# Three 128-row products of an FP32 token kernel split into 64-row halves, one image per PSUM bank

## The reference, cut to what matters

```
x = x + conv(group_norm(x))              # relu(info) * sigmoid(mask), 256 products, 1x1 conv
t = tokens(x)                            # 64 channels per token
q, k, v = ln(t) @ Wq, @ Wk, @ Wv         # norm 1: over 64 channels of a token
m = linear_attention(q, k, v) @ Wm       # 8 heads of 8
m = ln(m) * g1 + b1                      # norm 2
h = relu(cat(ln(t), m) @ W1) @ W2
t = t + ln(t) + ln(h) * g2 + b2          # norm 3
t = t + moe(ln(t))                       # norm 4; 8 experts, top 2, 64 -> 128 -> 64
```

## Time and profile before

| | |
|---|---|
| median of 3 runs | 1406.1 us (1400.49 to 1411.07) |
| the profiled execution | 1401.63 us, its span 1399.8 us |
| PE busy | 1227.9 us, 88% |
| DVE busy | 849.5 us, 61% |
| ACT busy | 736.9 us, 53% |
| POOL busy | 363.0 us, 26% |
| mean granted TensorE clock | 0.938 |

### The profile page before, as it was taken

How to read it: one execution, slowest core, us unless ns; L and a number is a source line. 1 busy time by engine, 2 the same in 40 slices (tenths; PEclk the granted TensorE clock), 3 DMA queues, 4 the chain that set the end, 5 groups by cost and what they waited for, 6 DMA issues and landing times.

```text
span 1399.8 us, 17533 instructions
## 1 busy us (share of the span) xinstructions
PE 1227.9 (88%) x6006; PEld 606.4 (43%) x6006; DVE 849.5 (61%) x1749; ACT 736.9 (53%) x982; POOL 363.0 (26%) x276
## 2 busy tenths in 40 slices
PE   5786799989999799987999988997889979999787
PEld 2565246434545237352373434643346434544111
DVE  6537665585548765567555876556665585547423
ACT  3442474654664556644556547464474554665433
POOL 0100132222323232222312223222241222323355
PEclk9987799989999799988999999998999989999999
DMA  2010561009310292003810066100661009210570
GB/s 91 31 31 1 124 151 34 13 1 199 92 46 1 56 204 61 16 2 79 195 47 16 1 135 155 31 16 3 145 145 40 7 1 205 55 46 1 113 162 15
DMA packets 15440, 96.67 MB, mean 69 GB/s; under 512 B 2672, under 2 KB 4720, under 8 KB 11120
## 3 DMA queue, kind: packets, MB, share of 16 engines
q1 hardware_dynamic: 15344, 95.46, 29.2%
HBM read 77.62 MB, written 9.44 MB: 62 GB/s over the span
## 4 chain that ended last, share of the span: by engine, by line
PE 50%; DMA 19%; DVE 11%; ACT 11%; issue 6%; SPq 2%; DVEq 0%; POOLq 0%; POOL 0%; ACTq 0%
DMA out<-XB 17%; PE HP L560 13%; PE R L455 9%; ACT H L677 8%; PE R L433 5%; PE YC L571 5%; PE R L513 5%; PE R L539 2%; PE R L492 2%; SPq L353 2%; PE R L520 2%; PE R L474 2%; PE R L483 2%; DMA CWB<-gates_hbm 1%; DVE TM L968 1%
## 5 line engine op out<-in xcount | busy, mean ns | idle before, releaser
L715 POOL TENSOR_TENSOR XB<-TM,XB 128x512 f32<-128x512 f32 x256 | 325.7, 1277 | 975.7 <-DVE TM L968 975.6
L677 ACT ACTIVATE H<-HP,W 128x1024 f32<-128x1024 f32 x256 | 285.7, 1116 | 352.9 <-PE HP L560 352.4
L560 PE MATMUL HP<-XF,W1E 64*128 64x512 f32 x1024 | 303.3, 670 | 38.8 <-ACT H L677 38.2
L968 DVE SCALAR_TENSOR_TENSOR TM<-YC,B2S,CWB 128x512 f32<-128x512 f32 x256 | 189.9, 747 | 196.4 <-PE YC L571 158.7
L571 PE MATMUL YC<-H,W 128*64 128x512 f32 x1024 | 292.2, 650 | 10.2 <-DVE TM L968 8.4
L560 PEld LDWEIGHTS HP<-XF,W1E 64*128 64x128 f32 x1024 | 80.1, 192 | 203.6 <-ACT H L677 165.4
L835 DVE TENSOR_REDUCE SM<-T 128x8 f32<-128x512 f32 x128 | 85.6, 684 | 111.4 <-ACT T L627 111.4
L571 PEld LDWEIGHTS YC<-H,W 128*64 128x64 f32 x1024 | 52.3, 139 | 209.3 <-issue 129.2
L433 PE MATMUL R<-W,T 128*128 128x128 f32 x768 | 100.2, 287 | 18.9 <-DVE T L845 18.9
L433 PEld LDWEIGHTS R<-W,T 128*128 128x128 f32 x768 | 89.4, 148 | 48.9 <-DVE T L845 42.4
L627 ACT ACTIVATE T<-R 128x512 f32<-128x512 f32 x128 | 73.8, 598 | 42.2 <-PE R L455 41.1
(11 more groups left out here) (96 smaller groups left out, 1371.5 us busy)
## 6 DMA issues: line engine op xcount, KB each, us to landing
CWB<-gates_hbm SPq DMA_DIRECT2D x32, 1536.0 KB, 26.4
CWB<-gates_hbm SPq DMA_DIRECT2D x32, 512.0 KB, 14.6
X<-x SPq DMA_DIRECT2D x16, 512.0 KB, 3.3
BIG<-XN SPq DMA_DIRECT2D x32, 256.0 KB, 3.8
out<-XB SPq DMA_DIRECT2D x16, 512.0 KB, 2.8
W<-wpack SPq DMA_DIRECT2D x1, 1176.0 KB, 7.2
gates_hbm<-CWR SPq DMA_DIRECT2D x16, 64.0 KB, 1.6
W1E<-w1e SPq DMA_DIRECT2D x1, 512.0 KB, 8.5
```

What stands on the lines that cost most here:

```text
L560: last = mm(HP[:, half(k)], W1E[img(k), e, :], XF[img(k), p, s, half(c)], start=True, stop=True)
L677: f(H[:, u % 2, :, :].rearrange("p k t -> p (k t)"), HP[:, :], ACT.Gelu, bias=col(B1E + e))\
L715: nc.gpsimd.tensor_tensor(acc, TM[:, u % 2, :], acc, ALU.add).then_inc(acc_done, 1)
L968: v.scalar_tensor_tensor(out=TM[:, u % 2, :], in0=YC[u % 2][:, :], scalar=B2S[:, e % 2, e // 2:e // 2 + 1], in1=CWB[:, s, e, half(c)], op0 ...
```

## The change

`by_token` at the three places is replaced by `image_tiles`. For each block of 128 tokens it makes two matmuls in place of one: 64 rows of the array (one image's channels) by 128 tokens, moving the 64 x 64 block of that image. Image 0's 64 columns go to the first bank of `R[s]`, image 1's to the second, block after block. Key and value keep `by_token`.

The layout in `R[s]` is then image by image, where it was block by block, so a bank is complete only when the whole slot is. PE therefore waits for both pieces of a slot before it starts, and signals both at its end. `scale_images` reads a bank (one image) and writes T1 in the old layout, in runs of 64 elements with a stride of 128; the transposes that follow, over both banks, wait for both of its operations. Norm 3 stays as it was.

```diff
+                def image_tiles(s, src, weights):
+                    for j in range(TB):
+                        for k in range(2):
+                            last = mm(R[s][:, CH * k + C * j:CH * k + C * j + C], src[img(k), s, P * j:P * j + P],
+                                      weights[img(k), img(k)], start=True, stop=True)
+                    return last
+
                 def centre_1():
-                    for s, c in PIECES:
-                        pe.wait_ge(x1_done, nth(a + 1, s, c))
-                        by_token(s, c, X, w("center")).then_inc(ln_ps, 1)
+                    for s in range(G):
+                        pe.wait_ge(x1_done, nth(a + 1, s, LAST))
+                        image_tiles(s, X, w("center")).then_inc(ln_ps, NCH)
...
                     for s, c in pieces(slots):
-                        pe.wait_ge(ln_tok, nth(a * LNS + k, s, c))
+                        if c == 0 or k == 3:
+                            pe.wait_ge(ln_tok, nth(a * LNS + k, s, c if k == 3 else LAST))
                         tokens(s, c, T1).then_inc(ln_back, 1)
...
                 def message():
-                    for s, c in PIECES:
-                        pe.wait_ge(att_done, nth(a + 1, s, c))
-                        by_token(s, c, T1, WMC[:, :]).then_inc(ln_ps, 1)
+                    for s in range(G):
+                        pe.wait_ge(att_done, nth(a + 1, s, LAST))
+                        image_tiles(s, T1, WMC).then_inc(ln_ps, NCH)
...
+                def scale_images(s):
+                    for k in range(2):
+                        v.tensor_tensor(T1[:, s, :].rearrange("p (j k c) -> p k j c", k=2, c=C)[:, k, :, :], norms(R[s][:, half(k)]),
+                                        SM[:, 3, s, some_norms(k)].unsqueeze(2)
+                                        .broadcast_to([P, NORMS // 2, C]), ALU.mult).then_inc(ln_tok, 1)
```

More of the change, by code:

```diff
@@ L529, in centre_4 @@
                 def centre_4():
-                    for s, c in PIECES:
-                        pe.wait_ge(x2_done, nth(a + 1, s, c))
-                        by_token(s, c, XB[:, par, :, :], w("center")).then_inc(ln_ps, 1)
+                    for s in range(G):
+                        pe.wait_ge(x2_done, nth(a + 1, s, LAST))
+                        image_tiles(s, XB[:, par, :, :], w("center")).then_inc(ln_ps, NCH)
                 def gates():
@@ L976, in parts @@
                     "conv_out": conv_out,
-                    "centre_1": lambda: squares(1), "rstd_1": lambda: rstd(1), "norm_1_0": lambda: scale(0), "norm_1_1": lambda: scale(1),
+                    "centre_1": lambda: squares(1), "rstd_1": lambda: rstd(1), "norm_1_0": lambda: scale_images(0), "norm_1_1": lambda: scale_images(1),
                     "query": lambda: elu_plus_one(1, Q), "key": lambda: elu_plus_one(2, K),
                     "key_value": key_value, "denominator": denominator, "numerator": numerator,
-                    "message": lambda: squares(2), "rstd_2": lambda: rstd(2), "norm_2_0": lambda: scale(0), "norm_2_1": lambda: scale(1),
+                    "message": lambda: squares(2), "rstd_2": lambda: rstd(2), "norm_2_0": lambda: scale_images(0), "norm_2_1": lambda: scale_images(1),
                     "tokens_3": lambda: squares(3), "rstd_3": lambda: rstd(3), "norm_3_0": lambda: scale(0), "norm_3_1": lambda: scale(1),
                     "features_3": features_3,
-                    "centre_4": lambda: squares(4), "rstd_4": lambda: rstd(4), "norm_4_0": lambda: scale(0), "norm_4_1": lambda: scale(1),
+                    "centre_4": lambda: squares(4), "rstd_4": lambda: rstd(4), "norm_4_0": lambda: scale_images(0), "norm_4_1": lambda: scale_images(1),
                     "gates": gates,
```

## The result

The changed kernel takes 1421.7 us (median of 4 runs, 1420.5 to 1427.9) against 1405.1 us before: a ratio of 1.0124, interval 1.0076 to 1.0173. Measured again beside the first experiments it was 1421.9 us, ratio 1.0104, interval 1.0084 to 1.0125. So it is 15 to 17 us slower. That is inside the forecast's range, but 12 us above the predicted time, and it is no "no change": both intervals lie wholly above 1, and both middles just beyond the 1% that the forecast drew as the line.

A forecast was written before the change was run, and what follows sets the result against it. Half of the span was PE, a fifth DMA; terms 0 + 0 + 1.2 + 3.9 + 0.5 + 1.1 = 6.7 us on 1401.6 gave 1408.3, on the median 1412.8, stated as 1410. Range 1396 to 1438.

The forecast's parts named there:

- the 1% that the forecast drew as the line: Whole kernel: about 1%, 14 us, tells a change from none; chance of staying within it 0.72.
- What sets the speed of the product: Centring and message products: weight loads set the time, two 64-row halves load together, product some 3.6 us, sum 0.
- The fast rival: The three products: 64-row loads take half as long, a product 1.8 us, the kernel 1380 us; chance 0.10.
- The slow rival of halves in turns: The three products: the halves' loads take turns, 3.6 us more each, 85 us in all, 1487; chance 0.10.
- Whole-slot waits: PE waiting for whole slots and both scalings: 1.2 at message, 3.9 in turn 0, 0.5 at features_1, 1.1 at features_4.
- One sign: Turn 0: transposes start 1.3 us later against the last square's start, since they wait for both scalings.
- The wait at `message`: PE waits for slot 0's last copy before the message product: some 0.15 us, eight times, 1.2 us.
- The wait at `features_4`: Slot 1's transposes wait for both scalings: 0.15 us in seven turns, 1.1 us.
- The squares in pairs: ACT gets both squares of slot 1 at the end; covered by the hidden layer, 0 in turns 1 to 7.
- the wait for the store: Turns 2 to 7: the second slot's query waits for ACT's XB behind a store; slack 0.63 to 1.74 us.
- The clock: Rival: granted clock falls behind the new products, 1.5 us at each of 18 exposed ones, 27 us, 1435; chance 0.08.
- the forecast's own range: Whole kernel, main case: 1398 (3 us gain, no waits) to 1422 (sum on the median, strided writes, more waits).

The follow-up runs named there:

- e4: Kernel before, each 128-column product at the three places split into two of 64 columns over all 128 rows: 1492.0 us, ratio 1.0603.
- e6: Changed kernel with image 0's centring and message products alone, image 1's left out: 1427.6 us, mean of two runs, 1419.4 and 1435.8.
- e5: Changed kernel with its two loops swapped, all eight blocks of image 0, then all eight of image 1: 1545.9 us, ratio 1.0986.
- e1: Kernel before with only the changed kernel's waits (whole slots at three products, transposes after both scalings), products unchanged: 1414.8 us, ratio 1.0057.
- e2: Changed kernel with two unused one-column matmuls (8 PE instructions) more ahead of the loop: 1412.7 us, ratio 1.0042.
- e7: Kernel before with the changed kernel's waits and 32 one-column matmuls (128 PE instructions) ahead of the loop: 1426.8 us, ratio 1.0154.
- e0: Changed kernel, unaltered, measured again as yardstick: 1421.9 us, ratio 1.0104.
- e3: Kernel before with 32 one-column matmuls (128 PE instructions) ahead of the loop: 1418.7 us, ratio 1.0081.

## Why the prediction was right or wrong

**What sets the speed of the product: right.** That 16 moving columns cost what 128 do and that two 64-row loads share their time gave 0 for the products; 30.3 us against 29.9, 30.7 and 31.6 is that. e4 and e6 show both halves of the argument. The fast rival, and with it the "up to 2x" of the Trainium skill's "TensorEngine Tiling (Array Packing)", "Theoretical Speedup", did not come: 64-row loads are no shorter than 128-row ones (29.2 us for 256 in e6, for 256 before). By the other page of the Trainium skill, "TensorE: Matmul & The Clock Gate", section "LDWEIGHTS", a load goes by its columns; the trace agrees, 29.2 us for either height.

**The slow rival of halves in turns: wrong for this kernel, right as a mechanism.** e5 is that rival, by the order alone, and cost 139 us where I had priced 85. Of the 54 us between them some 9 are the loop's start, which e5 shares with the changed kernel and the price left out; the rest goes with the lower clock, as far as is known.

**Whole-slot waits: right, a little small.** The sum was 6.7 us, e1 gives 8.0 (5.5 to 10.5). Turn 0 came at 3.2 us in the changed kernel's trace (133.04 against 129.82 for the gates) where I had 4.1. One sign was priced too high: the transposes of norm 1 in turn 0 were to start 1.3 us later against the last square's start and start 0.7 us later (50.22 - 44.95 = 5.27 us, against 49.27 - 44.70 = 4.57). The wait at `message` was 0.20 and not 0.15. The wait at `features_4` was 0.3 and not 0.15, seven times, 1 us in all and the largest miss here. The squares in pairs are covered, and `centre_1` and `features_1` vanish in the wait for the store, as the row in the changed kernel shows that answers to the earlier trace rows:

```profile
710.91 2.19 PE L459 MATMUL R<-XN,W 128*128 128x512 f32 x4 [1.05 <-ACT XB L645]
```

**The step that failed: the sum had no term for instructions.** I counted twice as many loads, weighed whether PE could be given four records in 0.11 us, and stopped there. That 384 more instructions ahead of the loop move its start, and that this start sets how long PE stands still at a back edge, was neither in the sum nor among the rivals. It is worth 5.7 us of waiting at the two back edges in the changed kernel (12.1 against 6.4), and 9.2 us in all by e2. With it the sum would have been 1401.6 + 6.7 + 9 = 1417 on the profiled execution, which took 1421.4. The medians split the measured 16 us in the same way: 9 us of waits (e1; 8.0 by the ratio), 9 us by the loop's start (e2 against the changed kernel), less the 2 us of the products (e2 against e1). That the second fetched block is what PE waits for is inferred from the counts of fetches; at which place in a block the loop begins no run shows.

**The hidden layer behind a product: not in the sum either.** It starts 0.15 us earlier, 14 x 0.15 = 2 us over the exposed products of turns 1 to 7, and e2 against e1 gives 2 us, itself within the noise. Why it does no run shows; presumably it is that both then use 64-row halves. e7 against the changed kernel gave 4 to 7 us, which is not clear of its noise.

**The clock: it fell in another place.** In the changed kernel no stretch at the lower clock follows the new products in turns 1 to 7, so the rival did not come. The mean is 0.925 and 0.932 in its two traces, 0.938 in the one before, but 0.928 to 0.936 in the other runs of the kernel before that the experiments brought, so the means differ by under 0.01. What changed is the stretch behind the longer idle time at the first back edge, 17.1 us at half of full speed where it was 10.2. After, then before:

```profile
628.90:646.00 17.10, 15.43 (x52) 9.43 (x52) 5.26 (x21) 5.21 (x5) 1.26 (x1) 0.50 0.00 1
```

```profile
617.80:628.00 10.20, 10.20 (x39) 7.05 (x38) 2.31 (x10) 2.34 (x2) 0.00 (x0) 0.50 0.00 1
```

There the gates' product takes 7.01 us, and 6.44 before. Followed unit by unit (by the starts of the gelu), the traces of e0 and e2 part by 4.1 us across the first back edge and by 3.2 across the second, of 7.5 us in all, where the waits alone differ by 3.7 and 2.3. Elsewhere the two drift apart and together again by up to 3 us. So in that pair some 1.4 us come on top of the waits right behind the edges, where the clock is low. In the pair of e3 and the kernel before it does not stay there: 8.1 of their traces' 22 us are at the back edges, and 2.9 us are one product of turn 0 at the lower clock (6.85 against 3.96 us). How much of what e2 and e3 show beyond the waits is clock in general stays open.

**The range** held the time, and so did the forecast's own range, by 0.3 us: it ended at 1422, with room for more waits than I saw. That is in part luck, since the sum lacked a term as large as all its others.

## What to carry to other kernels

Ask first whether a stream of matmuls goes by its loads or by its moving columns: compare it with a stream of the same loads and fewer columns. If it goes by loads, splitting it over row halves only keeps the time, and only if the halves' matmuls alternate; image by image it cost 9% of the kernel. And an edit that changes the number of instructions ahead of a loop also changes where the loop begins, which was worth 9 to 13 us of 1406 here: move it by a few instructions before judging the edit.

## What the runs showed of the hardware

- A loop's back edge costs PE 2.5 to 3.4 us without work in one set of kernels (before, e1, e2, e6) and 5.5 to 6.8 in another (changed, e0, e3, e4, e5, e7). One 16 KB block of instructions is fetched ahead of PE's first product behind the first back edge in the former and two in the latter, and the place where the loop begins decides: eight instructions more ahead of it brought 9.2 us back (e2).
- Two streams of 64-row loads on separate halves run at the pace of one, 0.114 us a pair (3.65 us for 32 pairs), also in runs of 32 and with 64 moving columns, with four records in that time.
- The order of the halves decides. Alternating, a product takes 3.8 us; one half after the other, 6.5 us and more, and the granted clock falls behind it (0.52 in the stretch shown). On all 128 rows such a stream takes 7.4 us, and the clock stays at 1.00 behind it (e4).
